# Attention scores from stacked bf16 parts that pass through DRAM, transposed scores straight into the exponential

## The reference

```python
normed = layer_norm(x, gamma1, beta1)
qkv = normed.reshape(b_, n_, H, HD).transpose(0, 2, 1, 3)      # H = 8 heads of HD = 16
scores = jnp.einsum('bhqd,bhkd->bhqk', qkv, qkv) / jnp.sqrt(HD)
masked = jnp.where(adj_matrix[:, None] > 0, scores, -jnp.inf)
attn = jax.nn.softmax(masked, axis=-1)
out = jnp.einsum('bhqk,bhkd->bhqd', attn, qkv)
x = x + out
```

## Time and profile before

| | us |
|---|---|
| runs of before: median (3 runs, 3308.73 to 3311.3) | 3308.82 |
| the profiled execution, its own time | 3315.0 |
| its span | 3312.9 |
| attention, from its first DMA issue to its last addition | 44.8 to 716.4 |

### The profile page before, as it was taken

How to read it: one execution, slowest core, us unless ns; L and a number is a source line. 1 busy time by engine, 2 the same in 40 slices (tenths; PEclk the granted TensorE clock), 3 DMA queues, 4 the chain that set the end, 5 groups by cost and what they waited for, 6 DMA issues and landing times. The chain is left out here.

```text
span 3312.9 us, 81916 instructions
## 1 busy us (share of the span) xinstructions
PE 2953.5 (89%) x26275; PEld 2586.8 (78%) x26402; DVE 2091.8 (63%) x6992; ACT 1629.6 (49%) x3020; POOL 1383.2 (42%) x1961
## 2 busy tenths in 40 slices
PE   3999999979989999999999987888862999997998
PEld 2999999979977777777777766777762999997787
DVE  4777777757766666666666654888873545443332
ACT  0444444435546666666666653555541444443443
POOL 2333333323322323232322222777773666665332
PEclk7999999989999999999999997887875999999999
DMA  1111111100000000000000000111142222221333
GB/s 37 42 42 38 38 38 39 40 11 0 0 1 0 0 0 0 0 0 0 0 0 0 0 2 28 56 53 55 56 127 68 77 77 77 77 81 56 111 104 89
DMA packets 166260, 126.10 MB, mean 38 GB/s; under 512 B 24246, under 2 KB 149689, under 8 KB 166202
## 3 DMA queue, kind: packets, MB, share of 16 engines
q1 hardware_dynamic: 148794, 89.43, 10.1%
q0 software_dynamic: 17408, 35.95, 3.2%
HBM read 68.36 MB, written 48.56 MB: 35 GB/s over the span
## 5 line engine op out<-in xcount | busy, mean ns | idle before, releaser
L780 POOL TENSOR_TENSOR s_sw<-s_expo,s_rsum 128x512 f32<-128x512 f32 x128 | 133.4, 1042 | 605.5 <-DVE s_rsum L1026 605.5
L1763 ACT ACTIVATE e_hidden<-e_ps,e_b1g 128x512 f32<-128x512 f32 x288 | 194.5, 687 | 257.6 <-PE e_ps L61 256.4
L394 ACT ACTIVATE a_prob<-a_prob 128x1024 f32<-128x1024 f32 x128 | 135.3, 1057 | 367.6 <-DVE a_prob L488 367.6
L1741 POOL DMA_INDIRECT token_y<-e_y,e_rows x288 | 282.5, 981 | 78.0 <-issue 68.3
L1226 POOL DMA_INDIRECT sorted_z<-r_z,r_rows x256 | 250.4, 978 | 84.9 <-issue 84.3
L1797 PE MATMUL e_ps<-expert_w,e_hidden 128*128 x2304 | 280.2, 275 | 0.0
L1797 PEld LDWEIGHTS e_ps<-expert_w,e_hidden 128*128 128x128 f32 x2304 | 273.8, 192 | 6.3
L434 PEld LDWEIGHTS a_ps_s<-a_headT,a_nT 128*128 128x128 f32 x2048 | 270.6, 193 | 8.7
L434 PE MATMUL a_ps_s<-a_headT,a_nT 128*128 128x128 f32 x2048 | 271.8, 276 | 0.0
L459 PEld LDWEIGHTS a_ps_o<-a_V,a_probT 128*128 128x128 f32 x2048 | 242.1, 194 | 0.8 <-issue 0.8
L459 PE MATMUL a_ps_o<-a_V,a_probT 128*128 128x17 f32 x2048 | 241.0, 260 | 0.7 <-DVE a_attn L479 0.7
(11 more groups left out here) (344 smaller groups left out, 8065.4 us busy)
## 6 DMA issues: line engine op xcount, KB each, us to landing
e_z<-sorted_z SPq DMA_DIRECT2D x72, 260.0 KB, 3.0
c_y<-token_y SPq DMA_DIRECT2D x32, 512.0 KB, 3.9
X<-in_x_dram SPq DMA_DIRECT2D x32, 256.0 KB, 2.9
a_adj<-in_adj_dram SPq DMA_DIRECT2D x32, 256.0 KB, 3.2
a_headT<-a_nT SPq DMA_DIRECT2D x256, 32.0 KB, 2.0
g_adj<-in_adj_dram SPq DMA_DIRECT2D x32, 256.0 KB, 2.9
out_dram<-X SPq DMA_DIRECT2D x32, 256.0 KB
token_y<-e_y,e_rows POOLq DMA_INDIRECT x288, 2.3
```

Source lines behind the costliest of these rows:

```text
L1741: nc.gpsimd.indirect_dma_start(sh.token_y, bass.IndirectOffsetOnAxis(ap=rows[p][:, b:b + 1], axis=0), y[p][:, b, :], None).then_inc(y_scat ...
L1763: nc.scalar.activation(hidden[p][:, c, :], ps_1[c % 2][:, :], ACT.Gelu, bias=b1g[p][:, c:c + 1]).then_inc(s["hidden_done"], 1)
```

## The change

Attention is rewritten; the other phases are untouched. In the words of the code:

- **Split parts.** ScalarE writes the normalised transpose twice, in f32 (`a_nT`) and as its bf16 rounding; VectorE makes two further bf16 parts of the rest (L466 and three instructions on VectorE). Channels are ordered (channel in head, head), by strided reads and by 32 small loads of `gamma1` and `beta1` at the start (L310).
- **Stacks.** SP stores the three parts of a group to a DRAM tensor `a_terms` (L342, 384 KB). From there it loads two bf16 tiles, `a_left` and `a_right`, in which six blocks of 16 partitions hold the parts: left 0,0,0,1,1,2 against right 0,1,2,0,1,0. One bf16 product over 96 partitions is then a head's score. A group's stacks are loaded in two halves (two graphs each), six transfers per half, in rows of 4 KB (L316, L319).
- **Scores twice.** TensorE makes the scores once for the maximum (L505, K = 96) and once transposed (L534, K = 99): in the second, three more rows subtract the maximum, itself split in three bf16 parts by GpSimd (L420 to L427), turned by TensorE (L513), copied out by ScalarE (L444) and put into `a_right` by a transfer of 6 KB per graph that ScalarE issues (L454).
- ScalarE takes the exponential of the transposed scores straight out of PSUM (L449). The subtraction on VectorE, the eight transposes and their copies are gone.
- TensorE multiplies with `a_V` as the stationary side, 17 columns (L553), ScalarE copies the result (L472), two transposes turn it back (L543). `X1` is written by ScalarE (L476) instead of VectorE. GpSimd makes `a_V` in two strided steps (L371, L377).
- Both score tiles in PSUM are single (`a_ps_s`, `a_ps_st`), where `a_ps_s` was double. The lag is one step longer (`LAG` 3 to 4).

The core of the diff, SP first:

```diff
-            def load(t, p):
-                sp.dma_start(X[:, bass.ds(t * GB, GB), :], x_g[t]).then_inc(x_loaded[p], 16)
-                sp.dma_start(adj[p][:, :, :], adj_g[t]).then_inc(adj_loaded[p], 16)
-
-                sp.wait_ge(nT_done, t)
-                for h in range(HEADS):
-                    rows = slice(h * HD, (h + 1) * HD)
-                    sp.dma_start(headT[1 - p][rows, h, :], nT[1 - p][rows, :]).then_inc(headT_loaded[1 - p], 16)
+        STACKS = ((0, 3), (3, 2), (5, 1))
+        K, PARTS, HALF = 6 * HD, 3, 2 * T
...
+        @block.sync
+        def _(sp):
+            sp.dma_start(X[:, 0:GB, :], x_g[0]).then_inc(x_loaded[0], 16)
+
+            for d in range(HD):
+                for tile, gamma in ((gcol, norm["gamma1"]), (bcol, norm["beta1"])):
+                    sp.dma_start(tile[d * HEADS:(d + 1) * HEADS, :], gamma.rearrange("(h d) -> h d", d=HD)[:, d:d + 1],
+                                 allow_slow_non_contiguous=True).then_inc(s["columns"], 16)
+
+            def stack(own, half):
+                for term, (block, n) in enumerate(STACKS):
+                    rows = slice(block * HD, (block + n) * HD)
+                    sp.dma_start(left[own][rows, half, :, :],
+                                 terms[own][term:term + 1, half, :, :, :].to_broadcast([n, HD, HEADS, HALF]))\
+                      .then_inc(ab_loaded[own][half], 16)
+                    sp.dma_start(right[own][rows, half, :, :],
+                                 terms[own][0:n, half, :, :, :].rearrange("t d h n -> t d (h n)"))\
+                      .then_inc(ab_loaded[own][half], 16)
+
+            def step(t, r, p, known):
+                q = 1 - p
+                for b in range(GB):
+                    kk, k = graph(t, b, known)
+                    if b == 0 and live(known, 2, groups):
+                        if since(known, 4):
+                            sp.wait_ge(s["st_done"], t * 4 - 12)
+                        stack(p, 1)
+                    if b == 1 and live(known, -1, groups):
+                        at, rows = X[:, bass.ds((t + 1) * GB, GB), :], x_g[t + 1]
+                        if since(known, 1):
+                            sp.wait_ge(s["stats_done"], t)
+                        sp.dma_start(at, rows).then_inc(x_loaded[q], 16)
+                    if b == 2 and live(known, 0, groups):
+                        if since(known, 2):
+                            sp.wait_ge(s["bias_done"], t - 1)
+                        sp.dma_start(adj[p][:, :, :], adj_g[t]).then_inc(adj_loaded[p], 16)
+                    if b == 2 and live(known, 1, groups):
+                        sp.wait_ge(s["split_done"], t)
+                        sp.dma_start(terms[q].rearrange("t a d h n -> (d h) (t a) n"),
+                                     split[q][:, :, :, :].rearrange("p t a n -> p (t a) n"))\
+                          .then_inc(stored[q], 16)
+                    if b == 3 and live(known, 1, groups):
+                        if since(known, 3):
+                            sp.wait_ge(s["st_done"], t * 4 - 10)
+                        sp.wait_ge(stored[q], (r + p) * 16)
+                        stack(q, 0)
+            run_steps(sp, step, groups - 2, LAG + 2, PEEL)
```

TensorE's part, ScalarE's transfer, and the split on VectorE:

```diff
-                            nc.tensor.matmul(S[:, 4 * c:4 * c + 4, :], sh.ident_bf[:, :],
-                                             edge_bias[p][:, b:b + 1, :].to_broadcast([T, 4, T]),
-                                             start=True, stop=False)
-                            for h in range(4 * c, 4 * c + 4):
-                                last = nc.tensor.matmul(S[:, h, :], nT[p][:, b * T:(b + 1) * T],
-                                                        headT[p][:, h, b * T:(b + 1) * T],
-                                                        start=False, stop=(h == 4 * c + 3))
...
+                        nc.gpsimd.tensor_tensor(z[:, 1, :], z[:, 3, :], z[:, 0, :], ALU.mult)\
+                          .then_inc(s["rstd_step"], 1)
+                        pool.wait_ge(s["rstd_step"], t * 7 + 7)
+                        nc.gpsimd.tensor_tensor(z[:, 2, :], z[:, 1, :], sh.eps[:, 0:GB], ALU.add)\
+                          .then_inc(s["rstd_done"], 1)
+                    if live(kk, 5, n_graphs):
...
+                        if since(known, 2):
+                            act.wait_ge(s["split_done"], t - 1)
+                        if since(known, 3):
+                            for half in range(2):
+                                act.wait_ge(ab_loaded[q][half], (r - 1 + p) * AB)
+                        nc.scalar.activation(nT[:, :], ps_n[:, :], ACT.Identity, bias=bcol[:, 0:1],
+                                             scale=gcol[:, 0:1])
+                        nc.scalar.activation(split[q][:, 0, :, :], ps_n[:, :], ACT.Identity, bias=bcol[:, 0:1],
+                                             scale=gcol[:, 0:1]).then_inc(s["nT_done"], 1)
...
+                        act.wait_ge(s["maxT_done"], k)
+                        own, i = (p, 0) if b == 3 else (q, b + 1)
+                        act.dma_start(right[own][K:K + PARTS, i // 2, :, (i % 2) * T:(i % 2 + 1) * T],
+                                     topsT[(b + 1) % 2][:, :])\
+                          .then_inc(max_loaded[(b + 1) % 2], 16)
+                    if b == 0 and live(known, 1, groups):
...
+                            act.wait_ge(s["split_done"], t - 1)
+                        if since(known, 3):
+                            for half in range(2):
+                                act.wait_ge(ab_loaded[q][half], (r - 1 + p) * AB)
+                        nc.scalar.activation(nT[:, :], ps_n[:, :], ACT.Identity, bias=bcol[:, 0:1],
+                                             scale=gcol[:, 0:1])
+                        nc.scalar.activation(split[q][:, 0, :, :], ps_n[:, :], ACT.Identity, bias=bcol[:, 0:1],
...
+                        last.then_inc(s["stats_done"], 1)
+                    if b == 1 and live(known, 2, groups):
+                        dve.wait_ge(adj_loaded[p], r * 16)
+                        if since(known, 4):
+                            dve.wait_ge(s["st_done"], t * 4 - 12)
+                        nc.vector.tensor_scalar(edge_bias[p][:, :, :], adj[p][:, :, :], 0.0, MASKED,
+                                                ALU.is_le, ALU.mult).then_inc(s["bias_done"], 1)
+                    if b == 1 and live(known, 0, groups):
+                        dve.wait_ge(s["stats_done"], t + 1)
```

More of the change, by code:

```diff
@@ L246, in sb, with two, ps @@
             return ctx.enter_context(nc.sbuf_tensor(name, shape, dt))
+        def two(name, shape, dt=F32):
+            return [sb(f"{name}{i}", shape, dt) for i in range(2)]
+        def ps(name, shape):
+            return ctx.enter_context(nc.psum_tensor(name, shape, F32))
         X, X1 = sh.X, sh.X1
-        adj = [sb(f"a_adj{i}", [T, GB, T], I32) for i in range(2)]
-        edge_bias = [sb(f"a_edge_bias{i}", [T, GB, T], BF16) for i in range(2)]
+        STACKS = ((0, 3), (3, 2), (5, 1))
@@ new lines, in attention_phase @@
+        n0 = two("a_n0", [T, GB, D])
+        nT = sb("a_nT", [D, W])
+        split = two("a_split", [D, 3, 2, HALF], BF16)
+        left, right = (two(f"a_{n}", [K + PARTS, 2, HEADS, HALF], BF16) for n in ("left", "right"))
+        terms = [nc.dram_tensor(f"a_terms{i}", [3, 2, HD, HEADS, HALF], BF16, kind="Internal").ap() for i in range(2)]
+        V = two("a_V", [T, GB, HEADS, HD + 1])
+        top = two("a_top", [T, HEADS])
+        top_rest = sb("a_top_rest", [T, HEADS])
+        tops = two("a_tops", [T, PARTS, HEADS], BF16)
@@ L296, in attention_phase @@
+        ab_loaded = [[sem(f"a_ab_loaded{i}{j}") for j in range(2)] for i in range(2)]
+        stored = [sem(f"a_stored{i}") for i in range(2)]
+        AB = 16 * 2 * len(STACKS)
         block = ctx.enter_context(nc.Block())
@@ L452, in step @@
[L452 to L461 removed]
+                            last = nc.tensor.transpose(ps_n[:, i * T:(i + 1) * T], n0[q][:, i, :], sh.ident[:, :])
@@ L465, in _ @@
         def _(dve):
+            for i in range(2):
+                nc.vector.memset(left[i][K:K + PARTS, :, :, :], -1.0)
+            nc.vector.memset(ps_ot[:, :, :], 0.0).then_inc(s["constants"], 1)
             def step(t, r, p, known):
+                q = 1 - p
                 for b in range(GB):
[L468 to L471 removed]
```

421 lines of the change are left out of this document (223 added, 198 removed).

## The result

The changed kernel takes **3589.35 us** (median of 4 runs, 3585.95 to 3597.76), the kernel before 3308.78 (3308.35 to 3311.3) on the same chip: a ratio of **1.085** (95% interval 1.083 to 1.087), 8.5% slower. The profiled execution took 3597.76 us, its span is 3596.0; the prediction's own sum for a profiled execution was 3598. The attention stage now ends with the addition at 1004.1 us, where it began its last one at 716: +288 us. The whole profiled execution grew by 283 (from 3315.0), so the change in time is this stage's; what follows it was some 5 us shorter.

What follows compares the result with a forecast made beforehand. TensorE bounded the kernel before; afterwards the few DMA engines carrying the stacks would, at 28.5 us a group for 19.96. The stage then ends at 1000 instead of 716 us, +283 on 3315.0, giving 3598, as a median 3592; range 3465 to 3685.

Steps and rivals of the forecast that it cites:

- case C: Attention's stack transfers, repeated and plain, run on 3 and 2 DMA engines: slower, 3592 us; chance 81%.
- Three and two DMA engines: Stack transfers are cut along their outermost DRAM count, 3 or 2, always onto the same low engines; 66 rows per half.
- The rate, 25.4 GB/s: Busiest DMA engine loads the stacks at its peak-slice rate: 10.65 us per half, 21.3 for two.
- The gap, 2.6 us, and the sum of 28.5: Engine runs dry between store and second six, once per group; 21.3 + 4.0 + 0.6 + 2.6 = 28.5 us per group.
- the small packets: 512-byte packets of `X`, `a_adj` and the store at 0.036 us each: 4.0 us per group; maxima add some 0.6.
- The engines, 16.4 us a group: Attention group by engine work alone: TensorE 14 us, VectorE 10.5, GpSimd 13.5; some 16.4 with a little for waits.
- Rival A: All 16 DMA engines share the stacks, so TensorE and GpSimd set 16.4 us a group: 3210 us, faster; chance 15%.
- First scores at 84 us: Attention's start: small loads issued 0.5 us apart, last landed at 63; first scores at 84 where they came at 65.
- Stage end at 1000 us: Attention stage ends at 1000 us instead of 716, +283 us; other phases do not change.
- A lower clock is covered: At half its clock TensorE's 14 us per group would be 28, just covered by the transfers.
- The maxima's transfer costs nothing: ScalarE's transfer of the maxima is used two graphs later, so its 2 us from issue to landing cost nothing.
- What would show it: Expected profile signs: period near 28.5 us, TensorE waiting for stacks, slow landings, DMA share about 0.2 at some 85 GB/s.

Runs made afterwards that it cites:

- outer16: Changed kernel with the DRAM pattern of each stack transfer leading with 16 instead of 3 or 2, same six transfers per half: 3275.2 us.
- rows16: Changed kernel with each stack transfer of 48 or 32 rows written as transfers of 16 rows, 12 per half instead of 6: 3278.43 us.
- left16: Changed kernel with only the loads of `a_left` cut into transfers of 16 rows: 3421.24 us.
- right16: Changed kernel with only the loads of `a_right` cut into transfers of 16 rows: 3412.02 us.
- early: Changed kernel with the split's three passes on VectorE put ahead of the third maximum: 3597.49 us.
- bal16: outer16 with GpSimd's values, root and maxima split spread over a group's four turns, and start work moved to ScalarE and VectorE's idle time: 3220.37 us.
- best16: tops16 with the root chain's second half in the next graph's turn and the stacks' minus ones written by ScalarE instead of VectorE: 3314.97 us.
- tops16: outer16 with GpSimd's four passes that split the maxima put ahead of values, root and addition in each graph's turn: 3319.31 us.
- spmax: Changed kernel with the maximum's transfer issued by SyncE instead of ScalarE, first in each turn: 3594.73 us.
- spmax16: outer16 with the maximum's transfer issued by SyncE instead of ScalarE, first in each turn: 3273.01 us.
- left16_early: left16 with the split put ahead of the third maximum on VectorE: 3398.98 us.

## Why the prediction was right

It forecast 3592 us in a range of 3465 to 3685 with 81% on case C; 3589.35 was measured. The mechanism is the one that was forecast. That the point is met within 3 us is luck beside it, since several terms of the sum are off and cancel. Step by step:

- **Three and two DMA engines** (C). Shown. The share of 0.14 to 0.20 in the middle of a group, 66 rows in 10.87 us, and above all outer16 and rows16, which change only the leading count and take 314 us away. The Trainium skill states it in the same terms (DMA: Bandwidth & Descriptors, "Why a DMA increments its semaphore by 16 and not by 1"): the largest divisor up to 16 of the slowest dimension of both patterns. By that rule, these runs agree in every case tried, counts of 3 and 2 against 16, on both the repeated and the plain source; which engines they are, the lowest-numbered as the page has it, no view of these runs shows. That the transfers on three and those on two share engines follows from the spacing: apart, the busiest would hold 34 rows and need 5.6 us at 24.9 GB/s, not 10.87.
- **The rate, 25.4 GB/s.** 24.9 on the busiest engine while the changed kernel's second six passes. Right there, and too high for a mix in which all sixteen engines work on stacks (left16: 22.3 us of transfers for 19.8). It spoiled my expectations of left16 and right16.
- **The gap, 2.6 us, and the sum of 28.5.** The sum stands against 28.6 measured, and 28.73 in the group shown, but its parts do not. By its terms the first six should need 13.2 us from issue to use (0.6, 2.0 and 10.65), the second 10.65, and the small packets of `X`, `a_adj`, the store and the maxima 4.6 behind them. The timeline has 15.52 (502.65 to 518.17), 10.87 (to 529.04) and 2.34 (to 531.38). So the first half was priced 2.3 us too low and the small packets 2.3 too high, and the two cancel; what holds the first six longer was not tried. At the group's change there is a dry stretch, as forecast: the windows at 503 and 531 show a share of 0.00 and 0.01. The early run shows that the cause given is the right one: the store stands behind the loads in the queue, and it makes no difference when it is ready.
- **The engines, 16.4 us a group.** Their busy times came out as priced: in outer16, 372.97/500 of 18.7 us is 13.9 on TensorE (14 predicted), 295.72/500 is 11.1 on VectorE (10.5), 325.57/500 is 12.2 on GpSimd (13.5, of which 1.1 were for semaphores, which don't count as busy). A bf16 product of 128 columns is a little cheaper than the 0.07 us taken: in outer16 two masks start 0.45 us apart (507.43 and 507.88) with four products between them, (0.45 - 0.21)/4 = 0.06. But that the group would then take 16.4 us was wrong: the step "by the engines alone a group would take some 16.4 us, with a little for waits" left out that four engines hand each graph on in a fixed order, with one long piece of GpSimd's in the way. Above those 16.4 us a group of outer16 takes 2.3 more, one of bal16 0.8. Rival A's price was therefore off by 65 us (3210 for 3275), its sign was right.
- **First scores at 84 us.** 84.93, by two errors that cancel. The small loads are issued every 0.34 us, not every 0.5, and the last is out at 55.4 us rather than landed at 63. In its place stood what I had not counted: the minus ones of both stacks, written by VectorE ahead of the first statistics (53.61). The timeline of the changed kernel:

```profile
45.24 3.47 DVE L561 MEMSET a_left<- 3x4096 bf16 x1 [2.27 <-PEq L75]
49.51 3.47 DVE L561 MEMSET a_left<- 3x4096 bf16 x1 [0.80 <-issue]
```

  Taking them away brings the first store forward by 4.1 us (best16 against tops16), so they were on the path; in bal16, where ScalarE also issues half of the small loads, it is 6.7 (against outer16).
- **Stage end at 1000 us.** 1004.1; what follows the stage was 5 us shorter, so that the profiled execution's 3598 came out.
- **A lower clock is covered.** The granted clock is 0.76 over a group and 0.50, the lower of its two levels, in the window at 511, where TensorE idles. TensorE is busy 14.98 of 28.73 us, so it is covered, as costed.
- **The maxima's transfer costs nothing.** Shown by spmax and spmax16.
- **"What would show it".** The period, TensorE's wait for `a_right`, the slow landing (the first six take 15.5 us from issue to use) and SyncE's wait for `a_terms` came as named. The DMA share is 0.28 at 88 GB/s where I wrote 0.2 at 85.

## What to carry to other kernels

Before anything else is costed in a transfer, read the leading count of both its patterns: a stack built as (copies, rows, bytes) runs on as many DMA engines as there are copies, and the same bytes walked as (rows, copies, bytes) on sixteen. The total bandwidth of the profile hides this, since 87 GB/s looks like an idle queue; the share of the sixteen engines beside TensorE's wait, and the landing times of unrelated transfers on the same queue, give it away. And once such a queue is out of the way, a wait that names one engine need not go when its work is moved first: here that cost 44 us. What helped was that no turn of the slowest helper holds two long pieces, so ask who waits for the piece that is pushed back.

## What the runs showed of the hardware that I had not expected

- An issue on SyncE is not a fixed cost. With the narrow loads still under way, single issues take 3.0, 4.5 and 5.4 us instead of 0.4 to 0.7 (508.72, 515.84 and, in left16_early, 509.90). A wait that follows such an issue looks short, while the time is in the issue.
- What a DMA engine moves while it is busy is not one number: over all packets 19.4 GB/s in the changed kernel, 17.4 in rows16, 17.1 in left16_early (112 GB/s with a share of 0.41) and 14.1 in outer16. The same bytes in transfers of 16 rows (rows16) and in transfers of 16 times 3 or 2 rows (outer16) differ by a fifth in this and by 3 us in the kernel's time. What sets it was not tried.
- The small loads with one element in each of eight rows are issued faster (0.34 us apart) than the larger ones of the earlier trace rows (0.5).
